# Two more products of a cross network split into two parts on VectorE, with the product in PSUM and one bank taken from each of two outputs

## The chip, the cores and the metric

The kernel runs on one core of a Trainium2 chip. The metric is device microseconds of one execution; the median of three runs of the kernel before is 1050.86 us (1050.23 to 1051.23). PE is TensorE, PEld its weight loads, DVE VectorE, ACT ScalarE, POOL GpSimd, SP the engine whose queue issues the plain DMAs.

## The reference

Each of 1024 rows looks up 32 fields (one row of 16 numbers in each of 32 tables). A cross network of three layers works on x0 [batch, 32 fields, 16]; two dense layers and a dot product end it.

```python
for i in range(3):                                      # h = x0 for the first layer
    z = (x0[:, :, None, :] * h[:, None, :, :]).reshape(B, F * G, E)
    y = relu(einsum('oc,bce->boe', W[i], z) + b[i][None, :, None])      # 128 outputs
    x_keep, h = (y[:, :64], y[:, 64:]) if i < 2 else (y, y)
    xs.append(x_keep)
z = concatenate(xs, axis=1).sum(axis=2)                 # 64 + 64 + 128 numbers a row
h = relu(concatenate([z, dense_ctx], axis=1) @ W_top1 + b_top1)
h = relu(h @ W_top2 + b_top2)
return h @ W_top3
```

## The kernel before, in words

The batch is cut into 8 blocks of 128 rows, each block into 4 tiles of 4 embedding positions: 32 tiles of 512 columns (4 positions x 128 rows). An item (layer, n) is two chunks of 128 channels of one layer of one tile. VectorE multiplies the two factors of an item into a 128x1024 product; TensorE multiplies it by the weights and adds it up in PSUM.

There are two ways to do this in full precision. A WHOLE item is one float32 product in `prod` (a ring of four); each of its chunks is one float32 matmul, which the hardware runs as two instructions, so an item is four matmuls in the trace (line 643). A split item is rounded by ScalarE to a float32r copy `high` (line 864), the rest is subtracted into a float32r `low` (line 514 on GpSimd, line 1125 on VectorE), and TensorE runs high by the high weights, high by the low weights (both line 651) and low by the high weights (line 666): six matmuls in float32r. In the kernel before all of layers 0 and 1 and the item (2,6) are WHOLE, and the other seven items of layer 2 are split with GpSimd's subtraction. Only in the last slot, where no other layer is left, three items are subtracted by VectorE.

The program is a row of slots, one for each tile. Slot n works on layer 0 of tile n+1, layer 1 of tile n and layer 2 of tile n-1. The order of the items in it is written out by hand in `SLOT`, and every engine goes through it in this order:

(1,0) (1,1) (2,0) (1,2) (2,1) (1,3) (0,0) (2,2) TAIL (1,4) (0,1) (2,3) (1,5) (2,4) (1,6) (2,5) (1,7) (2,6) (2,7)

TensorE runs an item's low matmuls after the high ones (or the whole ones) of the next item, and it transposes the next tile's fields into `xT` after (2,4). ScalarE, beside the copies, writes the next layer's factors `h0` (after layer 0 is complete) and `h1` (after (1,7)) into PSUM with `go_on` (line 850), and keeps the other halves in `kept` with `keep` (line 856). VectorE adds these up (`add_kept`, lines 1144 for the first tile of a block and 1148) and adds up layer 2's output in `add_last` (lines 1156, 1161).

GpSimd also issues the lookups of the next block (line 504), 8 in each slot, in a fixed pattern between its subtractions. The slot in which a block's first fields are needed (one in four) is called a turn slot below: there ScalarE, after the copy of (2,2), waits for the last lookups to land, copies them to `emb` (line 828), repeats the fields (line 836), and only then makes the copies of TAIL, a half-width item that GpSimd subtracts in line 522. In a turn slot GpSimd has no lookup ahead of (2,0), two after (2,2), three after (2,5) and three after (2,7); in the other slots it has one ahead, one each after (2,2), (2,3) and (2,4), and two each after (2,5) and (2,7).

PSUM has eight banks: `y0`, `y1`, two for `y2`, two for `h0`, `h1`, `xT`. ScalarE's order in a slot before: ... copy of (2,4), wait for layer 0 and write `h0` and its kept half, copy of (2,5), copy `xT` out once it is transposed (`take_x`, line 844), copy of (2,7), `h1` and its kept half. VectorE calls `add_kept` after (1,1) and `add_last` after (2,3).

Of the kernel before, what the change touches and what calls it, by code (L numbers as in the profile page):

```python
# [30 lines left out]
ALU = mybir.AluOpType  # L31
AXIS = mybir.AxisListType
ACT = mybir.ActivationFunctionType
F32 = mybir.dt.float32
# [57 lines left out]
WHOLE2 = (2, 6)  # L92
LAST_BY_DVE = [(2, 2), (2, 5), (2, 7)]

ADD_KEPT_AFTER = (1, 1)
# [75 lines left out]
def dlrm_tower(nc, dense_ctx, ids, tables, w_top1, b_top1, w_top2, b_top2, w_top3,  # L171
# [8 lines left out]
    with ExitStack() as ctx:  # L180
# [24 lines left out]
        w1T = sb("w1T", [P, CHUNKS, P])  # L205
        w2T_high = sb("w2T_high", [P, CHUNKS, P], F32R)
        w2T_low = sb("w2T_low", [P, CHUNKS, P], F32R)
        w2T_whole = sb("w2T_whole", [P, ITEM, P])
# [35 lines left out]
        unsplit, low = [None], [None]  # L244
        for kind in SPLIT:
            unsplit.append([])
            low.append([])
            for r in range(RING[kind]):
                raw, raw_at = sb_at(f"unsplit{kind}{r}", [P, ITEM, COLS])
                unsplit[kind].append(raw)  # L250
                low[kind].append(over(f"low{kind}{r}", [P, ITEM, COLS], F32R, raw_at))
# [27 lines left out]
        y2 = [ps(f"y2_{p}", [P, COLS]) for p in range(2)]  # L279
        h0 = [ps(f"h0_{p}", [P, COLS]) for p in range(2)]  # L280
# [3 lines left out]
        prep = [bank[:, :].rearrange("p (a b) -> p a b", b=P) for bank in y2]  # L284
# [81 lines left out]
        first_shifted = [[y1, y2[0], y2[1], h1, h0[1]], [y2[1], h1, h0[1], y2[0], y2[0]]]  # L366
# [4 lines left out]
        unit_bank = {(1, 0, 0): y0, (1, 0, 1): y1, (1, 0, 2): h0[0], (1, 0, 3): h0[1],  # L371
                     (1, 1, 0): y1, (1, 1, 1): h0[0], (1, 1, 2): h0[1], (1, 1, 3): h1,
                     (2, 0, 0): xT, (2, 0, 1): y0, (2, 1, 0): xT, (2, 1, 1): y0,
                     (3, 0, 0): y2[0], (3, 1, 0): y2[1]}
# [106 lines left out]
        def _(pool):  # L481
# [27 lines left out]
            def split_low(s, item):  # L509
                e, kind = plan.entry(s, item), BY_POOL  # L510

                pool.wait_ge(s_high[kind], e + 1)
                r = plan.place(s, item, RING)
                pool.tensor_tensor(low[kind][r][:, :, :], unsplit[kind][r][:, :, :],  # L514
                                   high[kind][r][:, :, :].bitcast(F32), ALU.subtract).then_inc(s_low[kind], 1)
# [56 lines left out]
        def _(pe):  # L572
# [46 lines left out]
            def accumulator(s, layer):  # L619
                return y2[(s[1] - 1) % 2] if layer == 2 else (y0, y1)[layer]  # L620

            def begin_layer(s, layer):
# [5 lines left out]
                elif not isinstance(s[0], int) or number(s) >= 2:  # L628
                    pe.wait_ge(s_sum2, number(s) - 2 + 1)

            def multiply(s, item):
# [6 lines left out]
                if kind == WHOLE:  # L638
                    z = prod[plan.place(s, item, RING)]
                    pe.wait_ge(s_made[kind], e + 1)  # L640
                    for c in range(ITEM):
                        w = w2T_whole[:, c, :] if layer == 2 else (w0T, w1T)[layer][:, ITEM * n + c, :]
# [3 lines left out]
                else:  # L646
                    z = high[kind][plan.place(s, item, RING)]
                    pe.wait_ge(s_high[kind], e + 1)
                    for c in range(ITEM):
                        for w in (w2T_high, w2T_low):  # L650
                            pe.matmul(y[:, :], w[:, ITEM * n + c, :], z[:, c, :],  # L651
                                      start=(n == 0 and c == 0 and w is w2T_high), stop=False)

            def multiply_low(s, item):
# [9 lines left out]
                pe.wait_ge(s_low[kind], plan.entry(s, item) + 1)  # L664
                for c in range(ITEM):
                    last = pe.matmul(accumulator(s, layer)[:, :], w2T_high[:, ITEM * n + c, :],  # L666
# [53 lines left out]
            def top1(unit, col):  # L720
# [4 lines left out]
                return three_passes(unit_bank[unit][:, :], wt1_high[:, cols], wt1_low[:, cols],  # L725
                                    z_high[n][col][:, :], z_low[col][:, rows], stop=(col == 1))

            def top1_dense(unit):
                _, n, m = unit
                pe.matmul(unit_bank[unit][:, :], wt_dense_parts[:, P * m:P * (m + 1)],  # L730
                          dense_parts[:, TOP1 * n:TOP1 * (n + 1)], start=True, stop=False)

            def top2(unit):
# [7 lines left out]
                for c in range(TOP1 // P):  # L741
                    cols = slice(TOP2 * c + P * m, TOP2 * c + P * (m + 1))
                    of = TOP1 // P * n + c
                    last = three_passes(unit_bank[unit][:, :], wt2_high[:, cols], wt2_low[:, cols],
# [4 lines left out]
            def top3(unit):  # L749
# [4 lines left out]
                pe.wait_ge(s_sum2, TILES - 1 + n + 1)  # L754
# [47 lines left out]
        def _(act):  # L802
# [56 lines left out]
            def split_high(s, item):  # L859
# [15 lines left out]
            def slot(s):  # L875
# [4 lines left out]
                h0_after = (2, 4) if (2, 4) in items else None  # L880
# [29 lines left out]
                if LAST1 in items:  # L910
# [4 lines left out]
                    go_on(h1, y1, 0, bias1, s_h1)  # L915
                    keep(s, y1, 1, s_kept1)
# [24 lines left out]
            def relu(unit):  # L941
# [3 lines left out]
                bank = unit_bank[unit][:, :]  # L945
# [11 lines left out]
            def take_first(t):  # L957
                for n, c in enumerate(FIRST_ORDER):
                    act.wait_ge(s_first, len(FIRST_ORDER) * t + n + 1)
                    act.copy(shifted_tail[:, :] if c == GROUP else shifted[:, c, :], first_shifted[t][c][:, :]).then_inc(  # L960
# [23 lines left out]
        def _(dve):  # L984
# [39 lines left out]
            lows = {2 + GROUPS + g: w2T_low[:, GROUP * g:GROUP * (g + 1), :] for g in range(GROUPS)}  # L1024
            def dense_low():
# [9 lines left out]
            for n, home in enumerate(homes):  # L1035
# [13 lines left out]
                elif n in lows:  # L1049
                    if WHOLE2[1] // (GROUP // ITEM) == n - 2 - GROUPS:  # L1050
                        of = ITEM * WHOLE2[1] % GROUP
                        dve.tensor_copy(w2T_whole[:, :, :], source[:, of:of + ITEM, :])
                    dve.tensor_copy(home, source).then_inc(s_w_high, 1)

                    dve.wait_ge(s_w_high, sorted(lows).index(n) + 1)
                    dve.tensor_tensor(lows[n], source, home.bitcast(F32), ALU.subtract).then_inc(s_stored, 1)
                else:
# [25 lines left out]
            def multiply(s, item):  # L1083
# [18 lines left out]
                b = (xT, h0[t[1] % 2], h1)[layer]  # L1102
# [9 lines left out]
                if not isinstance(e, int) or e >= RING[kind]:  # L1112

                    dve.wait_ge(s_used[kind], e - RING[kind] + 1)
                r = plan.place(s, item, RING)
# [168 lines left out]
```

## Time and profile before

| what | value |
|---|---|
| timed runs, median (lowest to highest) | 1050.86 us (1050.23 to 1051.23) |
| the profiled execution: span from the first to the last instruction | 1048.4 us |
| median less that span (what lies around it; the profiled execution has no other time of its own) | 2.5 us |
| PE busy | 1008.3 us, 96% |
| DVE busy | 826.9 us, 79% |
| POOL busy | 815.7 us, 78% |
| ACT busy | 476.5 us, 45% |
| mean busy share of the DMA engines in most slices | 0.8 to 0.9 |
| mean granted TensorE clock | 0.993 |

A busy PE need not be at its peak, since the ends of matmuls are modelled; the distance from one start to the next tells what a matmul takes. GpSimd's issuing of lookups is partly shown as busy (0.94 us each) and partly as gaps of 0.3 us.

### The profile page before, as it was taken

What the parts mean: (1) busy time and instruction counts of PE and PEld (TensorE: products, weight loads), DVE (VectorE), ACT (ScalarE), POOL (GpSimd) and SP (SyncE); (2) the same over time, 40 slices, a digit from 0 to 9 for tenths busy, and PEclk for the clock granted to TensorE, in tenths of its full rate; (3) what the DMA queues carried; (4) which work ended last, traced back from release to release, by engine and by line L of the source; (5) the groups of instructions that cost most, each with busy time, mean ns of one, the idle gap of its engine ahead of it and who ended that gap; (6) DMA issues with size and microseconds to landing.
All of it is one profiled execution on the core that took longest, in us unless ns stands there. A gap on an engine that the chain in (4) does not pass through costs nothing.

```text
span 1048.4 us, 11722 instructions
## 1 busy us (share of the span) xinstructions
PE 1008.3 (96%) x3269; PEld 589.9 (56%) x3269; DVE 826.9 (79%) x757; ACT 476.5 (45%) x600; POOL 815.7 (78%) x524
## 2 busy tenths in 40 slices
PE   3788999999999999999999999999999999999988
PEld 3744555555555555555555555555555555555555
DVE  4466777898788977898789977897889977788882
ACT  2143544444444544444544544444444544443443
POOL 7658789887998789887989799887989765556640
PEclk9998999999999999999999999999999999999999
DMA  7099999888998888889998889888998888889000
GB/s 160 10 208 220 204 197 198 191 193 187 211 202 189 192 186 190 192 188 191 199 207 185 196 186 191 190 190 189 197 205 187 195 188 190 183 189 227 21 1 1
DMA packets 48629, 184.15 MB, mean 176 GB/s; under 512 B 17442, under 2 KB 22050, under 8 KB 28132
## 3 DMA queue, kind: packets, MB, share of 16 engines
q1 hardware_dynamic: 40420, 181.83, 79.1%
q0 software_dynamic: 8192, 2.11, 1.9%
q8 instruction: 8, 0.13, 0.1%
q14 instruction: 9, 0.07, 0.0%
HBM read 180.75 MB, written 3.15 MB: 175 GB/s over the span
## 4 chain that ended last, share of the span: by engine, by line
POOL 45%; PE 25%; issue 16%; DMA 7%; DVE 3%; ACT 2%; POOLq 0%; SPq 0%; ACTq 0%; DVEq 0%
POOL low L514 25%; POOL looked_up L504 17%; PE y L643 15%; PE y L651 6%; DMA looked_up<-in_tbl,ids_now 4%; PE y L666 3%; POOL tail_parts L522 2%; DVE unsplit L1117 1%; DMA spread<-xcols 1%; DMA xcols<-xrows 1%; DVE prod L1117 1%; DMA shifted<-xcols 1%; ACT emb L828 0%; ACT tail_high L888 0%; ACT tail L887 0%
## 5 line engine op out<-in xcount | busy, mean ns | idle before, releaser
L514 POOL TENSOR_TENSOR low<-unsplit,high 128x1024 fp32r<-128x1024 f32 x221 | 524.7, 2389 | 104.8 <-ACT high L864 103.2
L643 PE MATMUL y<-prod,w1T 128*128 128x512 f32 x1024 | 478.4, 595 | 2.5 <-ACT kept L856 2.1
L1117 DVE TENSOR_TENSOR prod<-spread,h 128x1024 f32<-128x1024 f32 x288 | 348.9, 1215 | 118.0 <-PE y L643 102.3
L864 ACT CAST high<-unsplit 128x1024 fp32r<-128x1024 f32 x224 | 234.0, 1045 | 238.0 <-DVE unsplit L1117 237.6
L1117 DVE TENSOR_TENSOR unsplit<-spread,h 128x1024 f32<-128x1024 f32 x224 | 271.9, 1214 | 46.1 <-ACT h L850 46.0
L504 POOL DMA_INDIRECT looked_up<-in_tbl,ids_now x256 | 248.4, 970 | 67.2 <-issue 57.5
L643 PEld LDWEIGHTS y<-prod,w1T 128*128 128x128 f32 x1024 | 192.8, 191 | 162.2 <-issue 140.0
L651 PE MATMUL y<-high,w2T_high 128*128 128x512 f32 x448 | 226.9, 506 | 4.3 <-ACT high L864 4.3
L666 PE MATMUL y<-low,w2T_high 128*128 128x512 f32 x448 | 202.5, 533 | 5.0 <-POOL low L514 4.7
L850 ACT ACTIVATE h<-y,bias 64x512 f32<-64x512 f32 x128 | 83.3, 651 | 210.9 <-PE y L643 210.1
L651 PE MATMUL y<-high,w2T_low 128*128 128x512 f32 x448 | 177.8, 397 | 0.0
L666 PEld LDWEIGHTS y<-low,w2T_high 128*128 128x128 f32 x448 | 84.2, 190 | 89.3 <-issue 60.5
L643 PE MATMUL y<-prod,w0T 128*128 128x512 f32 x256 | 120.3, 592 | 1.3 <-DVE prod L1117 1.3
L651 PEld LDWEIGHTS y<-high,w2T_high 128*128 128x128 f32 x448 | 84.8, 189 | 49.6 <-issue 29.9
L651 PEld LDWEIGHTS y<-high,w2T_low 128*128 128x128 f32 x448 | 84.9, 190 | 43.6 <-issue 29.2
L1117 DVE TENSOR_TENSOR prod<-shifted,xT 128x1024 f32<-128x1024 f32 x64 | 77.6, 1214 | 6.2 <-DMA shifted<-xcols 5.7
L643 PEld LDWEIGHTS y<-prod,w0T 128*128 128x128 f32 x256 | 48.4, 190 | 44.0 <-issue 40.0
L643 PE MATMUL y<-prod,w2T_whole 128*128 128x512 f32 x128 | 60.1, 592 | 0.0
L522 POOL TENSOR_TENSOR tail_parts<-tail,tail_high 128x512 fp32r<-128x512 f32 x32 | 41.1, 1284 | 21.1 <-ACT tail_high L888 21.1
L856 ACT ACTIVATE kept<-y,bias_kept 64x512 f32<-64x512 f32 x64 | 43.7, 682 | 1.6
L844 ACT COPY xrows<-xT 48x512 f32<-48x512 f32 x32 | 18.5, 579 | 47.0 <-PE xT L615 46.9
L1148 DVE TENSOR_TENSOR acc_kept<-acc_kept,kept 128x512 f32<-128x512 f32 x24 | 38.8, 1616 | 0.0
(119 smaller groups left out, 468.9 us busy)
## 6 DMA issues: line engine op xcount, KB each, us to landing
spread<-xcols SPq DMA_DIRECT2D x128, 1024.0 KB, 9.1
shifted<-xcols SPq DMA_DIRECT2D x120, 256.0 KB
shifted_tail<-xcols SPq DMA_DIRECT2D x120, 64.0 KB
looked_up<-in_tbl,ids_now POOLq DMA_INDIRECT x256
xcols<-xrows SPq DMA_DIRECT2D x32, 96.0 KB, 2.0
spread<-in_L_rec_W SPq DMA_DIRECT2D x3, 512.0 KB, 7.2
spread<-in_L_rec_W SPq DMA_DIRECT2D x1, 1024.0 KB, 11.4
wt<-in_W_top SPq DMA_DIRECT2D x2, 512.0 KB, 8.3
```

The costliest lines, as they stand in the source:

```text
L504: pool.indirect_dma_start(out=looked_up[:, f, :], out_offset=None, in_=tables[f][:, :], in_offset=bass.IndirectOffsetOnAxis(ap=ids_now[:, ...
L514: pool.tensor_tensor(low[kind][r][:, :, :], unsplit[kind][r][:, :, :], high[kind][r][:, :, :].bitcast(F32), ALU.subtract).then_inc(s_low[k ...
L522: pool.tensor_tensor(tail_parts[:, :], tail[:, :], tail_high[:, :].bitcast(F32), ALU.subtract).then_inc(s_tail_low, 1)
L643: last = pe.matmul(y[:, :], w, z[:, c, :], start=(n == 0 and c == 0), stop=(item in (LAST0, LAST1) and c == ITEM - 1))
L651: pe.matmul(y[:, :], w[:, ITEM * n + c, :], z[:, c, :], start=(n == 0 and c == 0 and w is w2T_high), stop=False)
L666: last = pe.matmul(accumulator(s, layer)[:, :], w2T_high[:, ITEM * n + c, :], z[:, c, :], start=False, stop=(item == LAST2 and c == ITEM - 1))
L844: act.copy(xrows[:, :], xT[0:XROWS, :]).then_inc(s_xrows, 1)
L850: last = act.activation(h[to, :], y[lanes, :], ACT.Relu, bias=bias[lanes, :])
L856: act.activation(kept[t[1] % KEPT][lanes, :], y[lanes, :], ACT.Relu, bias=bias_kept[lanes, :]).then_inc(s_kept, 1)
L864: act.copy(high[kind][r][:, :, :], unsplit[kind][r][:, :, :]).then_inc(s_high[kind], 1)
L1117: dve.tensor_tensor(z, x[:, ITEM * n:ITEM * (n + 1), :], b[:, :].unsqueeze(1).to_broadcast([P, ITEM, COLS]), ALU.mult).then_inc(s_made[kin ...
L1148: dve.tensor_tensor(acc_kept[:, :], acc_kept[:, :], z[:, :], ALU.add).then_inc(s_sum_kept, 1)
```

## The change

Items (1,5) and (2,6) are split as well, with VectorE's subtraction; in the last slot (2,6) goes to GpSimd. VectorE writes these products into `pair`, a tensor of two PSUM banks, from which ScalarE copies `high` and VectorE subtracts to `low`. In the last slot VectorE's three items use `pair` too. The two banks come from `y2` and `h0`, which get one each. So TensorE may begin a tile's (2,0) only when VectorE has added up the tile before, and `add_last` moves from after (2,3) to after (2,1); ScalarE may write `h0` only when VectorE has multiplied (1,7), and it now does so after item (1,7), which comes after `take_x` in its order. `keep` of layer 0 moves to the end of the slot, between `h1` and the `keep` of layer 1. `add_kept` moves from after (1,1) to after (1,3). The weights of (1,5) get a high and a low part; the whole weights of (2,6) fall away. Some banks of the first and last phases are renamed.

```diff
-WHOLE2 = (2, 6)
+DVE_ITEMS = [(1, 5), (2, 6)]
+DVE_SPLIT1 = 5
-ADD_KEPT_AFTER = (1, 1)
+ADD_KEPT_AFTER = (1, 3)
+ADD_LAST_AFTER = (2, 1)
...
-    if item[0] < 2 or item == WHOLE2:
-        return WHOLE
-    return BY_DVE if last and item in LAST_BY_DVE else BY_POOL
+    if item in (LAST_BY_DVE if last else DVE_ITEMS):
+        return BY_DVE
+    return WHOLE if item[0] < 2 else BY_POOL
...
-        y2 = [ps(f"y2_{p}", [P, COLS]) for p in range(2)]
-        h0 = [ps(f"h0_{p}", [P, COLS]) for p in range(2)]
+        y2 = ps("y2", [P, COLS])
+        h0 = ps("h0", [P, COLS])
...
+        pair = ps("pair", [P, ITEM, COLS])
+        halves = [pair[:, c, :] for c in range(ITEM)]
...
-                    pe.wait_ge(s_sum2, number(s) - 2 + 1)
+                    pe.wait_ge(s_sum2, number(s) - 1 + 1)
...
+                    w_high, w_low, of = (w1T_high, w1T_low, 0) if layer == 1 else (w2T_high, w2T_low, ITEM * n)
                     for c in range(ITEM):
-                        for w in (w2T_high, w2T_low):
-                            pe.matmul(y[:, :], w[:, ITEM * n + c, :], z[:, c, :],
-                                      start=(n == 0 and c == 0 and w is w2T_high), stop=False)
+                        for w in (w_high, w_low):
+                            pe.matmul(y[:, :], w[:, of + c, :], z[:, c, :],
+                                      start=(n == 0 and c == 0 and w is w_high), stop=False)
...
-                act.copy(high[kind][r][:, :, :], unsplit[kind][r][:, :, :]).then_inc(s_high[kind], 1)
+                if kind == BY_DVE and (not isinstance(e, int) or e >= RING[kind]):
+                    act.wait_ge(s_used[kind], e - RING[kind] + 1)
+                source = pair if kind == BY_DVE else unsplit[r]
+                act.copy(high[kind][r][:, :, :], source[:, :, :]).then_inc(s_high[kind], 1)
 
             def next_h0(s):
 
                 act.wait_ge(s_used[WHOLE], plan.entry(s, LAST0) + 1)
-                go_on(h0[(s[1] + 1) % 2], y0, 1, bias0, s_h0)
+                if LAST1 in plan.items(s):
+                    act.wait_ge(s_made[WHOLE], plan.entry(s, LAST1) + 1)
+                go_on(h0, y0, 1, bias0, s_h0)
+
+            def keep0(s):
+
...
-                h0_after = (2, 4) if (2, 4) in items else None
+                h0_after = LAST1 if LAST1 in items else None
...
                     go_on(h1, y1, 0, bias1, s_h1)
+                if LAST0 in items:
+                    keep0(s)
+                if LAST1 in items:
                     keep(s, y1, 1, s_kept1)
...
+                if kind == BY_DVE:
+
+                    if not isinstance(e, int) or e >= 1:
+                        dve.wait_ge(s_low[kind], e)
...
-                z = prod[r][:, :, :] if kind == WHOLE else unsplit[kind][r][:, :, :]
+                z = pair[:, :, :] if kind == BY_DVE else (prod if kind == WHOLE else unsplit)[r][:, :, :]
...
-                dve.tensor_tensor(low[kind][r][:, :, :], unsplit[kind][r][:, :, :],
+                dve.tensor_tensor(low[kind][r][:, :, :], pair[:, :, :],
                                   high[kind][r][:, :, :].bitcast(F32), ALU.subtract).then_inc(s_low[kind], 1)
...
-                    if item == (2, 3) and s[1] >= START:
+                    if item == ADD_LAST_AFTER and s[1] >= START:
                         add_last(after(s, -2))
```

## Rows read from the trace of the kernel before

**Rows 1.** The page: busy time, share of the span and instructions of each engine.
```profile
PE 1008.3 (96%) x3269; PEld 589.9 (56%) x3269; DVE 826.9 (79%) x757; ACT 476.5 (45%) x600; POOL 815.7 (78%) x524
```

**Rows 2.** PE in order of time (start, duration, line, tiles), stretches without waits.
```profile
978.58 0.39 PE L651 MATMUL y<-high,w2T_high 128*128 128x512 f32 x1
...
981.69 0.40 PE L651 MATMUL y<-high,w2T_high 128*128 128x512 f32 x1
...
1002.80 0.39 PE L651 MATMUL y<-high,w2T_high 128*128 128x512 f32 x1
...
1004.20 0.40 PE L651 MATMUL y<-high,w2T_high 128*128 128x512 f32 x1
```

**Rows 3.** One slot, transposes to transposes: length, busy PE/PEld/DVE/ACT/POOL, granted clock, DMA share, GB/s.
```profile
522.22:551.54 29.32, 29.32 (x92) 16.85 (x91) 22.67 (x22) 13.82 (x17) 25.82 (x17) 1.00 0.91 196
```

**Rows 4.** Waits of PE and of DVE from 127 to 833 us: total, times, longest.
```profile
PE y L666 <- POOL low L514: 1.9, 4, 0.6
DVE prod L1117 <- DMA shifted<-xcols: 1.4, 1, 1.4
```

**Rows 5.** The page: the chain that ended last, shares of the span by line.
```profile
POOL low L514 25%; POOL looked_up L504 17%; PE y L643 15%; PE y L651 6%; DMA looked_up<-in_tbl,ids_now 4%; PE y L666 3%; POOL tail_parts L522 2%; DVE unsplit L1117 1%; DMA spread<-xcols 1%; DMA xcols<-xrows 1%; DVE prod L1117 1%; DMA shifted<-xcols 1%; ACT emb L828 0%; ACT tail_high L888 0%; ACT tail L887 0%
```

**Rows 6.** POOL in order of time, around the turn slot of 480 us.
```profile
467.14 2.36 POOL L514 TENSOR_TENSOR low<-unsplit,high 128x1024 fp32r<-128x1024 f32 x1
...
470.94 0.94 POOL L504 DMA_INDIRECT looked_up<-in_tbl,ids_now  x1 [0.30 <-issue]
...
498.02 2.38 POOL L514 TENSOR_TENSOR low<-unsplit,high 128x1024 fp32r<-128x1024 f32 x1
...
505.28 7.06 POOL L514 TENSOR_TENSOR low<-unsplit,high 128x1024 fp32r<-128x1024 f32 x3
...
526.53 2.36 POOL L514 TENSOR_TENSOR low<-unsplit,high 128x1024 fp32r<-128x1024 f32 x1
...
532.54 7.08 POOL L514 TENSOR_TENSOR low<-unsplit,high 128x1024 fp32r<-128x1024 f32 x3
```

**Rows 7.** ACT in order of time, same stretch.
```profile
463.90 0.58 ACT L844 COPY xrows<-xT 48x512 f32<-48x512 f32 x1 [1.59 <-PE xT L615]
...
479.71 0.62 ACT L828 COPY emb<-looked_up 128x512 f32<-128x512 f32 x1 [1.64 <-DMA looked_up<-in_tbl,ids_now]
...
497.97 1.31 ACT L850 ACTIVATE h<-y,bias 64x512 f32<-64x512 f32 x2 [3.23 <-PE y L643]
499.31 0.68 ACT L856 ACTIVATE kept<-y,bias_kept 64x512 f32<-64x512 f32 x1
```

**Rows 8.** PE in order of time: item (1,7) of the slot before the turn slot.
```profile
466.75 1.88 PE L643 MATMUL y<-prod,w1T 128*128 128x512 f32 x4
```

**Rows 9.** DVE in order of time, from several places.
```profile
466.68 3.12 DVE L1144 COPY acc_kept<-kept 128x512 f32<-128x512 f32 x1
...
499.41 1.22 DVE L1117 TENSOR_TENSOR unsplit<-spread,h 128x1024 f32<-128x1024 f32 x1 [2.72 <-ACT h L850]
500.55 1.21 DVE L1117 TENSOR_TENSOR prod<-spread,h 128x1024 f32<-128x1024 f32 x1
...
525.72 0.68 DVE L1148 TENSOR_TENSOR acc_kept<-acc_kept,kept 128x512 f32<-128x512 f32 x1
...
555.03 3.38 DVE L1148 TENSOR_TENSOR acc_kept<-acc_kept,kept 128x512 f32<-128x512 f32 x1
...
1000.79 3.00 DVE L1125 TENSOR_TENSOR low<-unsplit,high 128x1024 fp32r<-128x1024 f32 x1
...
1014.63 1.21 DVE L1125 TENSOR_TENSOR low<-unsplit,high 128x1024 fp32r<-128x1024 f32 x1
```

**Rows 10.** Groups of instructions, shapes apart: busy time, mean ns, idle before.
```profile
L1161 DVE SCALAR_TENSOR_TENSOR acc_last<-y,neg_last,acc_last 128x512 f32<-128x512 f32 x24 | 17.8, 743 | 0.8 <-PE y L666 0.8
L864 ACT CAST high<-unsplit 128x1024 fp32r<-128x1024 f32 x224 | 234.0, 1045 | 238.0 <-DVE unsplit L1117 237.6
L1056 DVE TENSOR_TENSOR w2T_low<-y,w2T_high 128x512 fp32r<-128x512 f32 x4 | 2.8, 692 | 0.1
```

More of the change, by code:

```diff
@@ L242, in dlrm_tower @@
                          for kind in SPLIT]
[L244 to L251, printed above, removed]
+        unsplit, low = [], [None, [], [sb(f"low{BY_DVE}{r}", [P, ITEM, COLS], F32R) for r in range(RING[BY_DVE])]]
+        for r in range(RING[BY_POOL]):
+            raw, raw_at = sb_at(f"unsplit{r}", [P, ITEM, COLS])
+            unsplit.append(raw)
+            low[BY_POOL].append(over(f"low{BY_POOL}{r}", [P, ITEM, COLS], F32R, raw_at))
         kept = [sb(f"kept{p}", [P, COLS]) for p in range(KEPT)]
@@ L278, in dlrm_tower @@
         y1 = ps("y1", [P, COLS])
-        y2 = [ps(f"y2_{p}", [P, COLS]) for p in range(2)]
-        h0 = [ps(f"h0_{p}", [P, COLS]) for p in range(2)]
+        y2 = ps("y2", [P, COLS])
+        h0 = ps("h0", [P, COLS])
         h1 = ps("h1", [P, COLS])
         xT = ps("xT", [P, COLS])
-        prep = [bank[:, :].rearrange("p (a b) -> p a b", b=P) for bank in y2]
+        pair = ps("pair", [P, ITEM, COLS])
+        halves = [pair[:, c, :] for c in range(ITEM)]
+        prep = [bank.rearrange("p (a b) -> p a b", b=P) for bank in (y2[:, :], halves[0])]
         s_ids = sem("s_ids")
@@ L619, in accumulator @@
             def accumulator(s, layer):
-                return y2[(s[1] - 1) % 2] if layer == 2 else (y0, y1)[layer]
+                return (y0, y1, y2)[layer]
             def begin_layer(s, layer):
@@ L664, in multiply_low @@
                 pe.wait_ge(s_low[kind], plan.entry(s, item) + 1)
+                w_high, of = (w1T_high, 0) if layer == 1 else (w2T_high, ITEM * n)
                 for c in range(ITEM):
-                    last = pe.matmul(accumulator(s, layer)[:, :], w2T_high[:, ITEM * n + c, :],
+                    last = pe.matmul(accumulator(s, layer)[:, :], w_high[:, of + c, :],
                                      z[:, c, :], start=False, stop=(item == LAST2 and c == ITEM - 1))
@@ L729, in top1_dense @@
                 _, n, m = unit
-                pe.matmul(unit_bank[unit][:, :], wt_dense_parts[:, P * m:P * (m + 1)],
+                pe.matmul(unit_bank[unit], wt_dense_parts[:, P * m:P * (m + 1)],
                           dense_parts[:, TOP1 * n:TOP1 * (n + 1)], start=True, stop=False)
@@ L944, in relu @@
                 act.wait_ge(s_top, units_to(unit))
-                bank = unit_bank[unit][:, :]
+                bank = unit_bank[unit]
                 if layer == 1:
@@ L1101, in multiply @@
                 x = shifted if layer == 0 else spread[t[1] % 2]
-                b = (xT, h0[t[1] % 2], h1)[layer]
+                b = (xT, h0, h1)[layer]
                 if layer == 1:
@@ L1111, in multiply @@
                 e, kind = plan.entry(s, item), plan.kind(s, item)
-                if not isinstance(e, int) or e >= RING[kind]:
+                r = plan.place(s, item, RING)
+                if kind == BY_DVE:
+                    if not isinstance(e, int) or e >= 1:
+                        dve.wait_ge(s_low[kind], e)
+                    else:
+                        dve.wait_ge(s_first_rows, 2 * len(FIRST_ORDER))
+                elif not isinstance(e, int) or e >= RING[kind]:
                     dve.wait_ge(s_used[kind], e - RING[kind] + 1)
-                r = plan.place(s, item, RING)
-                z = prod[r][:, :, :] if kind == WHOLE else unsplit[kind][r][:, :, :]
+                z = pair[:, :, :] if kind == BY_DVE else (prod if kind == WHOLE else unsplit)[r][:, :, :]
                 dve.tensor_tensor(z, x[:, ITEM * n:ITEM * (n + 1), :],
```

45 lines of the change are left out of this document (27 added, 18 removed).

## The prediction

> **What bounds the kernel now.** I read the busy shares first. TensorE is busy for 96% of the span, VectorE and GpSimd for 79% and 78% [rows 1]. A windowed view of one slot, from transposes to transposes, shows the same: TensorE is busy in all of its 29.32 us at the full granted clock [rows 3]. So a slot costs what TensorE's instructions cost. The waits say how near the others are. Between 127 and 833 us, where six blocks are looked up, TensorE waits 1.9 us in all, every time for GpSimd's subtraction [rows 4]. VectorE waits for a DMA once, 1.4 us [rows 4], so loading isn't a bound. But the chain that ended last runs through GpSimd: 25% its subtractions, 17% its lookups, then the landing of the lookups [rows 5]. TensorE and that chain have nearly the same length. The order of time shows where they meet: GpSimd is behind after a turn slot, and catches up in the three others [rows 6].
>
> **What the change saves on TensorE.** Without waits, a split item goes from 1002.80 to 1004.20, 1.40 us. A whole and a split item together go from 978.58 to 981.69, 3.11 us, so a whole one takes 1.71 [rows 2]. A split item saves 0.31 us, two in a slot 0.62: 28.70 us instead of 29.32. There are 32 tiles, so 64 items: 19.8 us.
>
> **VectorE.** It gets two subtractions a slot. No row has one from PSUM at this width. Half as wide, one operand in PSUM, it takes 0.69 us [rows 10]; with both in SBUF at full width 1.21, or 3.00 where GpSimd was subtracting too [rows 9]. I take 1.21. The low end is 1.13, the distance of two products [rows 9]; the high one 3.00. The product written to PSUM has no row either: 1.22 is the SBUF form, and two half-wide instructions (1.38) bound it above. VectorE idles 2.72 us before (2,0) alone [rows 9], and this work lies there.
>
> The Trainium skill (SBUF — State Buffer, Who interferes with whom) says that a VectorE instruction with at most one SBUF input, outside the two-port modes, doesn't contend with GpSimd. By it the subtraction from `pair` is never 3.00. No row shows one beside a GpSimd subtraction, so the chance of the slow case below is left open.
>
> **ScalarE.** It makes two more copies, 1.05 us each [rows 10]. From PSUM half a width takes 0.58 on 48 lanes [rows 7], so between 1.05 and 1.16. It is 45% busy [rows 1]; the copies matter only by their place.
>
> **The new waits.** Call S the moment at which TensorE has issued the last matmul of (1,7). For the turn slot in the rows S = 466.75 + 1.71 = 468.46 [rows 8]. After it TensorE now does low (2,5) 0.47, the highs of (2,6) and (2,7) 0.93 each, low (2,6) 0.47, and wants low (2,7) at S + 2.80. (1,0), (1,1), the highs of (2,0), (1,2) follow, and it wants low (2,0) at S + 9.32.
>
> *`y2` with one bank.* `h1` starts 0.20 after S, and VectorE's (2,0) 1.44 after that (499.41 against 497.97) [rows 7, 9]. Then come (1,2) and (2,1) at 1.13 each, and `add_last` from S + 5.0 to 5.8 at 0.74 [rows 9, 10]. TensorE wants the bank at S + 6.5. The margin is 0.6 us; behind this wait TensorE's whole stream is queued. I cost it at nothing.
>
> *`kept` of layer 1.* `h1` takes 1.31 and each `keep` 0.68 [rows 7], so it ends at S + 2.8; TensorE loads the weights of (1,0) at S + 3.0. Nothing, except in the first tile, where 0.6 us more of it shows.
>
> *`h0` with one bank.* ScalarE writes it after `take_x`, which waits for the transposes. TensorE ends these 4.8 us before the next S; `xT` out takes 0.58, `h0` 1.31, the copies of (2,6) and (2,7) 1.05 each [rows 7, 10], so the last is done at about S - 0.6. Behind this wait stand VectorE's low (2,6), (1,0) and (1,1), and GpSimd's low (2,7). VectorE gets through by S + 1.7, when `h1` lets it go on anyway. GpSimd's 2.38 us then end at S + 1.7 or later; before it was 467.14 + 2.36, S + 1.04 [rows 6].
>
> *`add_kept` after (1,3).* It comes at S + 6.9, when GpSimd is subtracting. The same addition takes 0.68 when it meets only lookups and 3.38 when it meets a subtraction [rows 9]; before, VectorE was idle next anyway. Now (0,0) and (2,2) are behind it. In a slot without a turn GpSimd needs 3.65 us of lookups and 2.36 for (2,0) (528.89 to 532.54 and on) [rows 6]. The addition ends 0.6 later; (0,0) 1.13, (2,2) 1.22 and its copy 1.1 follow, so low (2,2) starts 10.0 us after the last low (2,7) ended. From there to the end of the next (2,7) it is 18.9 (528.89 less 505.28 + 4.7) [rows 6]. GpSimd thus takes 28.9 us a slot against TensorE's 28.7: it doesn't catch up, but slips 0.2.
>
> **Where the saving goes.** The turn slot begins with GpSimd at S + 1.7 to 2.4. The copy to `emb` came 10.2 us after low (2,7) (479.71 less 469.50) [rows 6, 7], so it comes at S + 11.9 to 12.6 instead of S + 11.25. If instead the copy into `acc_kept`, 3.12 us beside a subtraction [rows 9], holds (2,2) up, it is S + 12.2 to 12.9. I take 12.6. From there GpSimd has no gap: low (2,0) of the next slot ended at 505.28 + 2.35 = 507.63, 27.92 later [rows 6, 7]. So it arrives at S + 40.5, and TensorE wants it at 28.70 + 9.32 = S + 38.0. TensorE loses 2.5 us around each turn, in place of 0.3 (1.9 over six) [rows 4]. 2.2 x 6 = 13.2 us are given back. With the copy to `emb` not moved at all it would be 1.15, 0.85 x 6 = 5.1; with the addition's full delay on top of 12.6 about 3.4, or 18.6.
>
> **The ends.** In the last slot VectorE's first subtraction takes 3.00 us [rows 9] and TensorE waits behind it: 1.21 from `pair` saves 1.8. That (2,6) goes to GpSimd there ends before VectorE's last subtraction. The first three split items lie in the start, where TensorE waits for loads: 0.9 of the 19.8 isn't had. `kept` costs 0.6. The weights' preparation lies under the first lookups.
>
> Sum: -19.8 + 13.2 - 1.8 + 0.9 + 0.6 = -6.9. The span goes from 1048.4 to 1041.5; the median is 2.5 above, so 1050.9 to 1044.
>
> **The rivals.**
>
> *A: GpSimd keeps up.* For it speaks that it waits for ScalarE in most ordinary slots and TensorE hardly for it [rows 4]; against it the chain [rows 5] and the later low (2,7). Without any loss it is 1050.9 - 20.1 = 1031; with 5.1 given back 1036. Chance 0.22, 1030 to 1037.
>
> *The forecast*: 13.2 given back, 9 to 18. 1039.5 to 1048.5, chance 0.50.
>
> *B: the margins go too.* `kept` has 0.2 us and `add_last` 0.6. If one is overrun by 0.25 in each of 28 slots it is 7 more: 1051, no change. For it: both hang on ScalarE's `h1`; against: all terms are measured rows. Chance 0.16.
>
> *C: slower, by the subtraction of (2,6).* It runs when GpSimd starts (2,7). At 3.00 instead of 1.21 VectorE comes to (2,0) 1.8 later, `add_last` ends at S + 7.6, and TensorE stands 1.2 us in each of 28 slots: 33 us, of which the 13 around the turns fall away, 1064. It is slower than before from 0.85 us of lateness on. For it: 3.00 in the last slot [rows 9]; against: that one had both operands in SBUF. Chance 0.12.
>
> So 1044, range 1034 to 1051. About 0.2% is what a measurement of this kernel can tell. Faster: A and the forecast, 0.72; same: B, 0.16; slower: C, 0.12.
>
> **What would show it.** Slots of 28.7 us wherever no lookups run (after 833 us), with nine split items of 1.40. In each of six blocks TensorE waits for GpSimd's low around the turn, 2 to 3 us together. GpSimd's wait for ScalarE before low (2,2), some 1 us, in ordinary slots, with `add_kept` at about 1.9 us before it. `pair`'s subtractions at 1.2. TensorE never waits for `add_last`. I'd be wrong if GpSimd's low (2,7) ended before S + 1, if the lookups landed earlier than 8.7 us after the last was issued, or if TensorE's waits were named VectorE's.

## The result, and the profile after

The changed kernel is slower: 1082.59 us, median of 4 runs (1082.46 to 1084.17), against 1050.55 for the kernel before beside it, a ratio of 1.031 (1.029 to 1.032). The forecast was 1044.

The page of the changed kernel, its first part and four of its groups of instructions:

```profile
PE 1002.6 (93%) x3397; PEld 608.9 (56%) x3397; DVE 923.7 (85%) x821; ACT 543.6 (50%) x664; POOL 818.2 (76%) x525
...
L1156 DVE TENSOR_TENSOR low<-pair,high 128x1024 fp32r<-128x1024 f32 x66 | 80.8, 1224 | 82.0 <-ACT high L874 81.8
...
L1148 DVE TENSOR_TENSOR pair<-spread,h 128x1024 f32<-128x1024 f32 x66 | 80.5, 1220 | 0.0
...
L874 ACT CAST high<-pair 128x1024 fp32r<-128x1024 f32 x66 | 66.9, 1013 | 13.9 <-DVE pair L1148 11.0
...
L1179 DVE TENSOR_TENSOR acc_kept<-acc_kept,kept 128x512 f32<-128x512 f32 x24 | 69.8, 2908 | 0.0
```

TensorE is busy for 5.7 us less than in [rows 1], in a span 32 us longer: it has become one that waits. The new work on VectorE and ScalarE costs about what it was priced at: 1.224 and 1.220 us for the subtraction from PSUM and the product into it, 1.013 for the copy. One row is out of all proportion: an addition to `acc_kept` that takes 0.68 where nothing is in its way [rows 9] has a mean of 2.91 (1.62 in the kernel before).

The windowed view of four slots (a whole block, from transposes to transposes), and of one slot after the last lookups; columns as in [rows 3]:

```profile
480.51:511.99 31.48, 29.62 (x97) 17.28 (x96) 30.87 (x27) 17.52 (x21) 24.93 (x17) 1.00 0.87 197
511.99:542.43 30.44, 29.28 (x96) 17.44 (x95) 24.73 (x24) 15.97 (x19) 28.04 (x20) 1.00 0.95 203
542.43:572.39 29.96, 29.00 (x97) 17.52 (x95) 26.25 (x22) 15.97 (x19) 24.17 (x15) 1.00 0.75 159
572.39:603.74 31.35, 29.52 (x96) 17.34 (x95) 29.16 (x25) 14.92 (x18) 25.36 (x17) 1.00 0.80 177
880.23:908.95 28.72, 28.72 (x97) 17.59 (x95) 26.59 (x24) 15.96 (x19) 18.09 (x9) 1.00 0.89 201
```

Without lookups a slot takes 28.72 us, 0.60 less than [rows 3]: the split items save what they should. With lookups the four slots take 123.23, where four quiet ones would be 114.88, so 8.35 is lost in this block. The granted clock is 1.00, its full level, in all five. The waits name who is late:

```profile
PE y L672 <- POOL low L518: 39.1, 46, 1.6
...
PE y L656 <- DVE acc_last L1192: 1.8, 1, 1.8
```

```profile
POOL low L518 <- ACT high L874: 147.9, 63, 4.9
```

TensorE waits 39.1 us for GpSimd's subtractions in the whole run, 33.4 of it between 127 and 833 us, where it waited 1.9 before [rows 4]. Why GpSimd is late shows in the order of time, in the slot three after a turn. First GpSimd, then VectorE, ScalarE and TensorE:

```profile
460.46 0.94 POOL L508 DMA_INDIRECT looked_up<-in_tbl,ids_now  x1 [0.30 <-issue]
461.43 4.69 POOL L518 TENSOR_TENSOR low<-unsplit,high 128x1024 fp32r<-128x1024 f32 x2
470.10 2.38 POOL L518 TENSOR_TENSOR low<-unsplit,high 128x1024 fp32r<-128x1024 f32 x1 [3.98 <-ACT high L874]
...
461.46 5.22 DVE L1179 TENSOR_TENSOR acc_kept<-acc_kept,kept 128x512 f32<-128x512 f32 x1
466.61 1.21 DVE L1148 TENSOR_TENSOR prod<-shifted,xT 128x1024 f32<-128x1024 f32 x1
467.74 1.21 DVE L1148 TENSOR_TENSOR unsplit<-spread,h 128x1024 f32<-128x1024 f32 x1
...
468.98 1.04 ACT L874 CAST high<-unsplit 128x1024 fp32r<-128x1024 f32 x1 [8.14 <-DVE unsplit L1148]
...
472.54 0.72 PE L672 MATMUL y<-low,w2T_high 128*128 128x512 f32 x2 [1.27 <-POOL low L518]
```

GpSimd subtracts (2,0) and (2,1) back to back, until 466.12. The addition, issued at 461.46, ends at 466.68, 0.56 after *both*. Behind it stand (0,0) and the product of (2,2), then ScalarE's copy, and only then can GpSimd start low (2,2): it has stood idle for 3.98 us, and TensorE waits 1.27 us for the result. The addition takes 3.8 us in the slot two after a turn and the copy into `acc_kept` 3.5 in the turn slot; in the slot after the turn it meets lookups only and takes 0.69. The prediction had let it get in after the first of the two.

### The profile page after: what moved, and what is told of

The parts are those of the page before. It is cut to its first block, busy times and chain, and to the rows that moved or that the text cites. A ratio compares the mean times of both kernels' runs of the same rounds, so it can differ in the third digit from the quotient of the medians.

```text
span 1080.3 us, 12229 instructions
## 1 busy us (share of the span) xinstructions
PE 1002.6 (93%) x3397; PEld 608.9 (56%) x3397; DVE 923.7 (85%) x821; ACT 543.6 (50%) x664; POOL 818.2 (76%) x525
## 4 chain that ended last, share of the span: by engine, by line
POOL 36%; issue 22%; PE 21%; DVE 10%; DMA 5%; ACT 4%; SPq 2%; DVEq 0%; POOLq 0%; ACTq 0%
POOL low L518 23%; POOL looked_up L508 11%; PE y L647 9%; PE y L656 5%; DVE prod L1148 3%; PE y L672 3%; DVE unsplit L1148 2%; DMA xcols<-xrows 2%; DMA spread<-xcols 2%; POOL tail_parts L526 2%; PE xT L609 1%; DVE acc_kept L1175 1%; SPq L440 1%; ACT high L874 1%; ACT h L857 1%
## 5 line engine op out<-in xcount | busy, mean ns | idle before, releaser
L647 PE MATMUL y<-prod,w1T 128*128 128x512 f32 x896 | 417.1, 594 | 7.5 <-DVE prod L1148 4.8
L1148 DVE TENSOR_TENSOR prod<-spread,h 128x1024 f32<-128x1024 f32 x224 | 268.9, 1212 | 17.1 <-DMA spread<-xcols 15.5
L647 PEld LDWEIGHTS y<-prod,w1T 128*128 128x128 f32 x896 | 166.6, 190 | 149.7 <-issue 125.3
L672 PE MATMUL y<-low,w2T_high 128*128 128x512 f32 x512 | 212.2, 499 | 39.3 <-POOL low L518 39.1
L656 PE MATMUL y<-high,w2T_low 128*128 128x512 f32 x512 | 203.6, 398 | 0.0
L1156 DVE TENSOR_TENSOR low<-pair,high 128x1024 fp32r<-128x1024 f32 x66 | 80.8, 1224 | 82.0 <-ACT high L874 81.8
L656 PEld LDWEIGHTS y<-high,w2T_high 128*128 128x128 f32 x512 | 96.8, 189 | 50.2 <-ACT high L874 15.8
L656 PEld LDWEIGHTS y<-high,w2T_low 128*128 128x128 f32 x512 | 96.8, 189 | 38.9 <-issue 20.0
L1148 DVE TENSOR_TENSOR pair<-spread,h 128x1024 f32<-128x1024 f32 x66 | 80.5, 1220 | 0.0
L874 ACT CAST high<-pair 128x1024 fp32r<-128x1024 f32 x66 | 66.9, 1013 | 13.9 <-DVE pair L1148 11.0
L1179 DVE TENSOR_TENSOR acc_kept<-acc_kept,kept 128x512 f32<-128x512 f32 x24 | 69.8, 2908 | 0.0
```

Of the source, the lines that this page charges most:

```text
L647: last = pe.matmul(y[:, :], w, z[:, c, :], start=(n == 0 and c == 0), stop=(item in (LAST0, LAST1) and c == ITEM - 1))
L656: pe.matmul(y[:, :], w[:, of + c, :], z[:, c, :], start=(n == 0 and c == 0 and w is w_high), stop=False)
L672: last = pe.matmul(accumulator(s, layer)[:, :], w_high[:, of + c, :], z[:, c, :], start=False, stop=(item == LAST2 and c == ITEM - 1))
L874: act.copy(high[kind][r][:, :, :], source[:, :, :]).then_inc(s_high[kind], 1)
L1148: dve.tensor_tensor(z, x[:, ITEM * n:ITEM * (n + 1), :], b[:, :].unsqueeze(1).to_broadcast([P, ITEM, COLS]), ALU.mult).then_inc(s_made[kin ...
L1156: dve.tensor_tensor(low[kind][r][:, :, :], pair[:, :, :], high[kind][r][:, :, :].bitcast(F32), ALU.subtract).then_inc(s_low[kind], 1)
```

## The experiments

**The addition's place.** Undone alone (first); in another place, where GpSimd issues lookups (second); the same place with the second operand from PSUM, which leaves the sum of layers 0 and 1 out of the result (third); and, the other way round, the old kernel with nothing but that move (fourth).

```diff
 e1_add_back
-ADD_KEPT_AFTER = (1, 3)
+ADD_KEPT_AFTER = (1, 1)
 e3_add_in_lookups
-ADD_KEPT_AFTER = (1, 3)
-ADD_LAST_AFTER = (2, 1)
+ADD_KEPT_AFTER = (1, 2)
+ADD_LAST_AFTER = (1, 2)
...
-                    if item == ADD_LAST_AFTER and s[1] >= START:
+                    if item == ((2, 1) if plan.is_last(s) else ADD_LAST_AFTER) and s[1] >= START:
 e2_add_from_psum (in add_kept)
-                z = kept[t[1] % KEPT]
+                z = h1
 e6_only_add_moved (on the kernel before)
-ADD_KEPT_AFTER = (1, 1)
+ADD_KEPT_AFTER = (1, 3)
```

> add_kept goes back to after (1,1), all else as in the changed kernel. Theory L (an addition with both operands in SBUF waits until GpSimd's whole run of back-to-back subtractions has ended, which after (1,3) is 3.8 to 5.2 us): after (1,1) it meets at most the one subtraction of (2,7), so (0,0) and (2,2) are no longer held up, but (2,0) can come up to 2 us late; 1045 to 1062 us. Rival O (ScalarE's order and the single h0 bank make GpSimd's (2,7) late, the addition's place hardly matters): within 5 us of 1082.6. Rival Y (the single y2 bank): no better than 1082.6.

> Both additions after (1,2), add_kept ahead of add_last, the order of the last slot kept. Theory L: after (1,2) GpSimd issues lookups in most slots, so add_kept takes 0.7 us there, and (2,2) comes 3 to 4 us earlier than in the changed kernel; 1034 to 1046 us. In slots without lookups it may wait 1 to 2 us. Rival O: within 5 us of 1082.6. Rival Y (the sum of layer 2 frees the bank too late): add_last is at most 0.5 us earlier, so within 10 us of 1082.6.

> add_kept stays after (1,3) but reads the PSUM bank h1 instead of kept, so the sum of layers 0 and 1 is left out of the result; number, width and order of the instructions stay. Theory L: with one SBUF operand the addition takes 0.7 us beside subtractions too, GpSimd's wait before (2,2) falls from 4 us to about 1, and the time is 1034 to 1044 us, what was forecast for the change. Rivals O and Y: the single banks and the order are all still there, so 1075 us or more.

> The kernel before with one edit: add_kept after (1,3). No item more is split, and all banks are as before. Theory L: the additions meet runs of subtractions there too, 3 to 7 us, low (2,2) is late, and two or three of four slots take 31 us; 1065 to 1090 us. Rivals O and Y (the single banks of h0 and y2, the order that they force): both are absent here, so 1048 to 1053 us.

Measured: 1040.33 (ratio to the kernel before 0.990, 0.989 to 0.992), 1040.45 (0.990, 0.988 to 0.991), 1039.69 (0.990, 0.988 to 0.992), and 1080.04 (1.027, 1.025 to 1.029). The first is below its expected range: the additions, which were to wait for the one subtraction of (2,7), took 0.69 in the median. The others lie in theirs. The move of one addition costs the old kernel 29 us, and the changed one 42. The third says why. VectorE and GpSimd in the run with the PSUM operand:

```profile
416.67 0.69 DVE L1179 TENSOR_TENSOR acc_kept<-acc_kept,h 128x512 f32<-128x512 f32 x1
...
414.27 0.94 POOL L508 DMA_INDIRECT looked_up<-in_tbl,ids_now  x1 [0.30 <-issue]
415.24 4.73 POOL L518 TENSOR_TENSOR low<-unsplit,high 128x1024 fp32r<-128x1024 f32 x2
```

Same place, same run of two, and the addition takes 0.69 us: it is not late because of its position, but because both its operands lie in SBUF while GpSimd subtracts. The Trainium skill (SBUF — State Buffer, Who interferes with whom) has the rule: two SBUF inputs contend with a GpSimd instruction that reads SBUF, one does not. This run and the changed kernel agree with its two halves (0.69 against 5.22 us), and so does the subtraction from `pair`: none of the 66 takes more than 1.227.

**Another explanation, ScalarE's order**, that `take_x` ahead of `h0` makes everything late.

```diff
 e4_xT_late
-                x_after = (2, 5) if (2, 5) in items else None
+                x_after = (2, 7) if (2, 7) in items else None
```

> add_kept as in the changed kernel; ScalarE copies xT out after (2,7) instead of (2,5), so h0 and the copies of (2,6) and (2,7) no longer wait for the transposes. Theory L: GpSimd's (2,7) can come 1 to 3 us earlier where it waited for that copy, but the additions still wait for runs of two subtractions; 1072 to 1084 us. Rival O: 1050 to 1065 us, since this takes away the wait it blames. Rival Y: unchanged.

Measured: 1079.92 (1.028, 1.026 to 1.030). The additions still take 3.85 and 5.4 us. ScalarE's order is worth some 2.7 us; as the explanation of the 42 it falls.

**The run of two broken up** by moving a lookup between low (2,0) and low (2,1), in the three slots without a turn.

```diff
 e5_lookup_between
-LOOKUPS_AFTER = (..., (0, 0, 1, 1, 1, 2, 2))
+LOOKUPS_AFTER = (..., (1, 0, 0, 1, 1, 2, 2))
```

> The changed kernel; in the slots that aren't turn slots one lookup is moved from after low (2,2) to between low (2,0) and low (2,1) on GpSimd, their number per slot is the same. Theory R (the addition waits until GpSimd's run of back-to-back subtractions ends): it now gets in after low (2,0), so in two slots of a block it ends 2.4 us earlier; 1045 to 1060 us. Rival S (it waits for the whole of both because of where it was issued, or it is the number of subtractions ahead of (2,2) that counts): additions of 3.8 to 5.2 us stay, within 6 us of 1082.6.

Measured: 1062.53 (1.011, 1.009 to 1.012), a little above the range: 20 of the 42 us are won back. The additions take 1.5 us and end 0.56 after low (2,0). The turn slot still has its run, and its copy is still held for both. One slot of the profile, from 292.29 to 328.55 us, is 7.5 us longer than the same slot of the other blocks: GpSimd stands 5.64 us before a lookup there, and the trace shows no cause. Less these 7.5 us the profiled run, 1062.41, would lie in the range.

**Both remedies together**: `take_x` late and the additions among the lookups (the edits of e3 and e4).

> The two additions after (1,2) and xT copied out after (2,7), together. If the 1.2 us that TensorE still loses at each turn come from GpSimd's (2,7) waiting for ScalarE's copy behind the transposes (theory P), they fall by half or more: 1032 to 1038 us. If they come from the lookups and subtractions alone, which take GpSimd 28.5 us in the slot after a turn (rival Q), it is 1038 to 1042 us, as with the additions alone.

Measured: 1039.39 (0.989, 0.988 to 0.991), hardly better than the additions alone (1040.45): in rival Q's range and not in P's.

**The wait by itself.** "It waits for the whole run" was so far read from one kernel. The run e6 spoke against it. GpSimd and VectorE there, in a slot without lookups and in one with them:

```profile
884.95 5.16 POOL L514 TENSOR_TENSOR low<-unsplit,high 128x1024 fp32r<-128x1024 f32 x2 [4.60 <-ACT high L864]
...
887.10 0.77 DVE L1148 TENSOR_TENSOR acc_kept<-acc_kept,kept 128x512 f32<-128x512 f32 x1
...
548.42 0.95 POOL L504 DMA_INDIRECT looked_up<-in_tbl,ids_now  x1 [0.30 <-issue]
549.39 4.67 POOL L514 TENSOR_TENSOR low<-unsplit,high 128x1024 fp32r<-128x1024 f32 x2
...
550.51 4.11 DVE L1148 TENSOR_TENSOR acc_kept<-acc_kept,kept 128x512 f32<-128x512 f32 x1
```

In the first the pair of subtractions takes 5.16 in place of 4.67, and the addition got in between. So a kernel with nothing but such trials, every trial twice:

```python
# GpSimd                                  # VectorE
pool.wait_ge(s_go, k + 1)                 dve.wait_ge(s_go, k + 1)
for i in range(n):                        # products that read PSUM, as a delay
    if r and i == 1:                      for i, size in enumerate(d): ...
        pool.wait_ge(s_act, gate_to[k])   dve.tensor_tensor(acc_kept[:, :],
    pool.tensor_tensor(low[i], ...)           acc_kept[:, :], kept[:, :], ALU.add)
```

> This kernel measures the disputed wait by itself and leaves the whole computation of the reference out: its result is zeros. 18 trials, each twice. In a trial GpSimd subtracts a run of 128x1024 tensors (2.36 us each), VectorE, after a multiplication that reads PSUM and takes 0.65 to 1.8 us, adds two 128x512 SBUF tensors. Runs of 1, 2, 3 and 4 with nothing to wait for: the theory that the addition waits for the whole run (W) expects it to end 0.55 us after the run's end in each, so that it takes about 1.7, 4.1, 6.5 and 8.8 us from its issue at 1.2 us. The assumption of the prediction, that it waits for the one subtraction in progress (I), expects 1.7 us in all four. With the second operand in PSUM beside a run of four both expect 0.69; a copy of SBUF to SBUF beside a run of four should wait as the addition does. Then runs of two whose second subtraction has to wait for ScalarE, which is done 0.35, 1.05, 1.6 or 2.1 us after the first began, while the addition is issued at 0.65, 1.2 or 1.8 us. W1: the addition waits for both whenever the second is ready before the first ends, all twelve. W2: it waits for both only where the second was ready before the addition was issued, and gets in between otherwise. W3: it gets in between only where the second becomes ready less than some 1 us before the first ends, whenever the addition was issued: that is the cases of 1.6 and 2.1. In the run with the addition alone moved, 0.2 us before the end let it in and 1.2 us did not.

VectorE beside the runs of 2, 3 and 4 subtractions:

```profile
17.86 1.80 DVE L80 TENSOR_TENSOR acc_kept<-acc_kept,kept 128x512 f32<-128x512 f32 x1
23.10 1.80 DVE L80 TENSOR_TENSOR acc_kept<-acc_kept,kept 128x512 f32<-128x512 f32 x1
30.64 1.80 DVE L80 TENSOR_TENSOR acc_kept<-acc_kept,kept 128x512 f32<-128x512 f32 x1
```

Beside a run of one it took 1.87, beside the longer ones no more. W falls, and so do W1, W2 and W3: all twelve trials with a wait in the run were let in after the first subtraction too (1.2 to 2.34 us, by when the addition was issued). Here the prediction's assumption holds. What has the kernel that the trials had not?

```python
for f in range(look):          # e9: lookups ahead of the run
    look_up(f)
if gap:                        # e9: and time between them
    pool.wait_ge(s_act, act_to[k + 1])
for i in range(n): ...         # in place, or not; after 4 MB of plain loads, or not
for f in range(behind):        # a lookup behind the run
    look_up(3)
```

> Alone on the chip the addition got in after the one subtraction in progress, even beside a run of four (1.80 us from its issue), so the theory that it waits for a whole run falls as it stands: something that the kernel has and those trials had not must make it wait for two. In the kernel each run of two that held the addition for both began right behind a lookup; the slots without lookups let it in after one. This kernel, which also leaves the whole computation out, repeats the trials with one thing added at a time. Each trial: GpSimd's lookups if any, then a run of subtractions of 2.36 us; VectorE's addition is issued in the first of them, or later where it says so. Theory K (a lookup ahead): with one or three lookups straight ahead of the run the addition waits for two or more subtractions, 4 us or more from its issue, and without a lookup for one, under 2.4 us. Theory D (traffic): it waits for two where 4 MB are being loaded by plain DMAs meanwhile, with no lookup. Theory A (in place): it waits for two where the subtraction writes over its own input, as it does in the kernel. Theory B (behind): it waits for two where a lookup stands behind the run. Under K a gap of 3 us between the lookup and the run tells whether the lookup must be straight ahead. If all trials give under 2.4 us, none of the four is the cause, and it stays open. With the second operand in PSUM all expect 0.69.

GpSimd and VectorE with one lookup ahead of a run of three and of four; then in place, without a lookup:

```profile
178.07 0.96 POOL L120 DMA_INDIRECT looked_up<-in_tbl,ids_now  x1 [0.86 <-ACTq L110]
179.04 6.93 POOL L133 TENSOR_TENSOR low<-unsplit,high 128x1024 fp32r<-128x1024 f32 x3
180.10 6.44 DVE L94 TENSOR_TENSOR acc_kept<-acc_kept,kept 128x512 f32<-128x512 f32 x1
186.84 0.96 POOL L120 DMA_INDIRECT looked_up<-in_tbl,ids_now  x1 [0.86 <-ACTq L110]
187.82 9.23 POOL L133 TENSOR_TENSOR low<-unsplit,high 128x1024 fp32r<-128x1024 f32 x4
188.87 8.72 DVE L94 TENSOR_TENSOR acc_kept<-acc_kept,kept 128x512 f32<-128x512 f32 x1
...
292.36 1.80 DVE L94 TENSOR_TENSOR acc_kept<-acc_kept,kept 128x512 f32<-128x512 f32 x1
```

K it is. A lookup straight ahead makes the addition wait for the whole run, 8.72 us for four, ending 0.54 after it. In place and a lookup behind the run (1.80 each) are not the cause. With time between lookup and run it was 2.59, one subtraction. With the operand in PSUM 0.68; a copy from SBUF to SBUF is held too, 6.17.

The trial with plain loads gave 1.80 as well, but says nothing of traffic: SyncE issued the loads when the trial before was done on VectorE, and by 284.5 us, when the addition of the second such trial (284.83) was still to come, they were over. The run e6 answers it. Windows of the two, e9 without TensorE's columns and e6 with them, otherwise as in [rows 3] (the last number is GB/s):

```profile
284.50:286.70 2.20, 2.13 (x2) 0.00 (x0) 2.20 (x2) 1.00 0.00 0
...
884.95:890.11 5.16, 5.16 (x15) 2.65 (x14) 5.16 (x6) 1.05 (x1) 5.16 (x2) 1.00 1.03 224
```

At 887.10 us the addition of e6 got in after one subtraction (0.77, above) while plain loads moved 224 GB/s. So traffic without a lookup doesn't hold it.

**What breaks the hold.** Between lookup and run a tiny memset, or a wait of several lengths; a plain DMA in the lookup's place; a wait inside the run.

```python
for f in range(plain):                     # e11
    pool.dma_start(fetched[:, :], table[0:P, :])
for f in range(small):
    pool.memset(tiny[:, :], 0.0)
if gap:                                    # ahead of the run
    pool.wait_ge(s_act, act_to[k + 1])
for i in range(n):
    if gate and i == 1:                    # inside the run
        pool.wait_ge(s_act, act_to[k + 1])
    pool.tensor_tensor(low[i], ...)
```

> This kernel again leaves the whole computation out. A lookup, then a run of three subtractions, held the addition for all three (6.44 us); without the lookup, or with some microseconds between, it waited for one. Here: a tiny memset on GpSimd between lookup and run; a plain DMA issued by GpSimd in the place of the lookup; gaps between lookup and run of about 0.2, 0.4, 0.9 and 1.4 us (the run waits for ScalarE); and a wait for ScalarE between the first and the second subtraction that is over 0.4, 0.9, 1.4 or 1.9 us after the first began. If the lookup must be straight ahead (K1), any gap and the memset give 1.8 to 2.6 us; if the run is held because GpSimd has its instructions ready while the lookup runs (K2), the memset doesn't help (6.4), a gap does, and a wait between first and second does too where it is over late (under 2.6 us), while one that is over early doesn't. If the hold is a matter of the time since the lookup (K3), the gaps help only from some length on. Last, an addition issued while the lookup's run is about to begin, and two additions in a row, of which the second should take 0.7.

The trials with the memset, with the plain DMA, and with the shortest gap:

```profile
142.21 0.11 POOL L125 MEMSET tiny<- 128x1 f32 x1
142.26 6.94 POOL L131 TENSOR_TENSOR low<-unsplit,high 128x1024 fp32r<-128x1024 f32 x3
143.28 6.47 DVE L89 TENSOR_TENSOR acc_kept<-acc_kept,kept 128x512 f32<-128x512 f32 x1
150.09 0.58 POOL L123 DMA_DIRECT2D fetched<-in_tbl  x1 [0.89 <-ACTq L103]
150.69 6.94 POOL L131 TENSOR_TENSOR low<-unsplit,high 128x1024 fp32r<-128x1024 f32 x3
152.10 6.09 DVE L89 TENSOR_TENSOR acc_kept<-acc_kept,kept 128x512 f32<-128x512 f32 x1
...
159.72 7.39 POOL L131 TENSOR_TENSOR low<-unsplit,high 128x1024 fp32r<-128x1024 f32 x3 [0.24 <-ACT prod L105]
161.13 1.49 DVE L89 TENSOR_TENSOR acc_kept<-acc_kept,kept 128x512 f32<-128x512 f32 x1
```

Neither K1 (the memset doesn't help) nor K2 (a wait over as late as 1.8 us into the first subtraction doesn't either, 6.45) was right whole, and nothing speaks for K3: 0.24 us of idling, the shortest tried, is enough. What fits every trial is that behind a DMA that GpSimd issues, lookup or plain, VectorE is kept out until GpSimd next stands idle. In e5 the 0.16 us before a lookup inside the run did it too. A wait that is already over when GpSimd comes to it is no idling. An addition issued 0.08 us before the run began was held for all of it, 7.56; a second addition behind a held one, with the run over, took 0.68.

**The prediction's assumption made true in the kernel.**

```diff
 e10_pool_lets_in
                 pool.wait_ge(s_high[kind], e + 1)
+                if item == (2, 1) and s[1] >= START:
+                    pool.wait_ge(s_sum_kept, number(s) - 1)
```

> The changed kernel with one more wait: GpSimd begins the subtraction of (2,1) only when VectorE's addition is done. The addition stays after (1,3), so this makes true what the prediction assumed, that it waits for the one subtraction in progress: it should end 0.55 us after low (2,0) and take 1.5 to 2.9 us in place of 3.8 to 5.2, GpSimd should wait for it some 0.6 us and then about 1 us before low (2,2) in place of 3.7 to 4.0. If the second subtraction that it waited for is the whole cost (K, a run behind a lookup is not let go between its members): 1040 to 1047, the prediction's own range for its forecast. If additions at this place cost time for another reason too (N), 1055 or more.

TensorE's (1,7) ahead of a turn slot and GpSimd's run in the slot after that one; then GpSimd and VectorE in the slot three after a turn:

```profile
469.00 1.88 PE L649 MATMUL y<-prod,w1T 128*128 128x512 f32 x4
...
508.66 7.07 POOL L520 TENSOR_TENSOR low<-unsplit,high 128x1024 fp32r<-128x1024 f32 x3
...
446.97 0.95 POOL L508 DMA_INDIRECT looked_up<-in_tbl,ids_now  x1 [0.31 <-issue]
447.94 2.39 POOL L520 TENSOR_TENSOR low<-unsplit,high 128x1024 fp32r<-128x1024 f32 x1
451.02 2.39 POOL L520 TENSOR_TENSOR low<-unsplit,high 128x1024 fp32r<-128x1024 f32 x1 [0.70 <-DVE acc_kept L1181]
454.30 2.39 POOL L520 TENSOR_TENSOR low<-unsplit,high 128x1024 fp32r<-128x1024 f32 x1 [0.88 <-ACT high L876]
...
449.02 1.86 DVE L1181 TENSOR_TENSOR acc_kept<-acc_kept,kept 128x512 f32<-128x512 f32 x1
```

Measured: 1046.31 (0.995, 0.994 to 0.997). The addition ends 0.55 us after low (2,0), and GpSimd's wait before low (2,2) falls from 3.98 to 0.88. One more wait makes the changed kernel 36 us faster and puts it into the forecast's own range of 1039.5 to 1048.5.

## Why the prediction was wrong

The step that failed is "*`add_kept` after (1,3)*": "The addition ends 0.6 later", that is, 0.6 after low (2,0). It ends 0.56 after low (2,1), one subtraction later. The 3.38 us that it was sized by (555.03) [rows 9] had been an addition beside a run of one. It could not show what a run of two behind a lookup does, and the prediction took a wait for one subtraction to be the rule. In the row of before where VectorE did get in between subtractions (1000.79, 3.00 us) [rows 9], no lookups were left, as in the first trials above; the row was no warning. GpSimd's rows at these two places of the kernel before:

```profile
555.50 2.36 POOL L514 TENSOR_TENSOR low<-unsplit,high 128x1024 fp32r<-128x1024 f32 x1
...
997.97 8.09 POOL L514 TENSOR_TENSOR low<-unsplit,high 128x1024 fp32r<-128x1024 f32 x3 [1.30 <-ACT high L864]
```

From there the prediction's own working leads on: (0,0), (2,2) and its copy follow, and low (2,2) starts 4.0 us after low (2,1) ended in place of the 0.9 that e10 shows. GpSimd, which had 28.9 us of work against 28.7, now takes 31.3 to 31.5 in the turn slot and the slot before it. It doesn't catch up while lookups run.

With that step mended, and nothing else, e10 is 1046.3 against the forecast of 1044. The other steps, by their numbers:

- *TensorE's saving*: slots of 28.72 against 28.70.
- *VectorE and ScalarE's new work*: 1.224, 1.220 and 1.013 against 1.21, 1.22 and 1.05 to 1.16, so the copy is a little cheaper.
- *One bank for `y2` and for `kept`*: costed at nothing, except 0.6 for `kept` in the first tile. In the changed kernel TensorE waited for `acc_last` once, 1.8 us, in the whole run; with the addition back in its place (e1) it did seven times, 5.0 us in all, so the margin is thin.
- *The turn*: "TensorE loses 2.5 us around each". In e10, the only run where it can be read, the four slots of the block from 404.62 to 522.00 take 117.38, which is 2.5 more than 4 x 28.72; over the six blocks it is 2.0 to 2.9. It comes as forecast: S is there 469.00 + 1.71 = 470.71, and GpSimd's low (2,0) of the slot after the turn ends at 508.66 + 2.36, which is S + 40.3 against S + 40.5.
- *Rival A* (GpSimd keeps up, 1030 to 1037) is nearly reached once the additions are out of GpSimd's way: 1039 to 1040 in e1, e2, e3 and e7. A block still loses some 1.3 us, most of it in one slot of 29.9 (e1) or 30.0 (e3) instead of 28.7, and TensorE's waits for GpSimd are 7 to 10 us in all.
- *Rival C*, the only slower one, had the right kind of wait and the wrong instruction: the subtraction from `pair` has one operand in SBUF and is never held. The addition has two.

That the range was too low follows from this: every rival let a stretched instruction cost at most what a row of before had shown, 3.4 us, though the change moved the addition to a place where GpSimd's subtractions come in runs of two.

What is open: why a DMA issued by GpSimd has this effect. The runs show when the hold begins and ends, not what is held.

## What to carry to other kernels

Where GpSimd issues DMAs, an addition of VectorE with both operands in SBUF can cost the rest of GpSimd's run, up to GpSimd's next pause (5.22 us in place of 0.68 here). So before moving one, look up what GpSimd does back to back at the new place, and what stands behind the instruction on VectorE. Where it can't be moved, one operand in PSUM (0.69 us in place of 5.22) or a semaphore that makes GpSimd stand idle for a moment (36 us here) lets it in. The fastest kernels of the study with the whole result are the change with the addition back in its place (e1) and with both additions moved among the lookups (e3, e7), 1039.4 to 1040.5 us, 1% below the kernel before and not told apart: the two split items were worth having, and the new place of one addition hid it.

## What was not expected of the hardware

Behind a DMA that GpSimd issues itself (an indirect lookup or a plain DMA), a VectorE addition or copy with its operands in SBUF was kept out through every GpSimd instruction that followed without a pause: 4.15, 6.44 and 8.72 us for runs of two, three and four 128x1024 subtractions. Without that DMA it got in after the one in progress, 1.80 us beside a run of four. An idle time of 0.24 us on GpSimd ended the hold; a memset of one column in its place did not. The Trainium skill (SBUF — State Buffer, SBUF: two separate sides) says that whichever of the two starts first has the shared ports for the whole instruction, and the other is blocked. The runs without a DMA ahead agree (1.80 us beside a run of four), the runs behind one do not (8.72).
